# Pooling each batch row in its own 32 by 32 tile of TensorE, with a second gather of the fields as the weights and a matmul with ones as the sum

## The reference

```python
e = jnp.stack([tbl_0[ids[:, 0]], ..., tbl_32[ids[:, 32]]], axis=1)      # 512 x 33 x 128
row, col = np.triu_indices(33, k=1)
inner = x[:, row] * x[:, col]                                           # 512 x 528 x 128
fm = jax.nn.relu(jnp.einsum('bpd,ad->bpa', inner, attn_W) + attn_b)
scores = jnp.einsum('ba,bpa->bp', gnn_feature, fm)
attn = jax.nn.softmax(scores, axis=1)
attn_output = jnp.einsum('bp,bpd->bd', attn, inner) * 100.0
h = jnp.concatenate([gnn_feature, attn_output, r_gnn_feature], axis=1)
h = jnp.maximum(h @ W_top1 + b_top1, 0.0)
h = jnp.maximum(h @ W_top2 + b_top2, 0.0)
y = h @ W_top3
```

## Time and profile before

| | |
|---|---|
| median of 3 runs | 608.61 us (608.36 to 609.79) |
| the profiled execution: its own time, its span | 609.33 us, 607.5 us |
| TensorE matmul busy | 591.5 us (97%) |
| DVE busy | 567.9 us (93%) |
| ACT busy | 504.0 us (83%) |
| POOL busy | 235.6 us (39%) |
| share of the chain that ended last | PE 80%, DVE 10%, issue 3%, DMA 3%, ACT 2% |

### The profile page before, as it was taken

One profiled execution on the slowest core, in us unless ns is written; L12 is line 12 of the kernel. 1 busy time (PEld: TensorE's weight loads), 2 busy tenths in 40 slices (PEclk: granted clock), 3 DMA queues, 4 the chain that ended last, 5 costly groups with the idle time before them and its releaser, 6 DMA issues.

```text
span 607.5 us, 24776 instructions
## 1 busy us (share of the span) xinstructions
PE 591.5 (97%) x10754; PEld 401.6 (66%) x10754; DVE 567.9 (93%) x793; ACT 504.0 (83%) x1068; POOL 235.6 (39%) x215
## 2 busy tenths in 40 slices
PE   7999999999989999999999999999899999999887
PEld 5555555556669899555567789655467777556456
DVE  5699999999989999999999999999999999999963
ACT  2889899889988878889999878898899878887841
POOL 6688878864323333444423333443100122021010
PEclk9999999999999999999999999999999999999999
DMA  3212311151341113100071111200030011510250
GB/s 96 55 40 93 92 33 41 37 29 21 22 30 22 38 30 30 15 21 15 20 29 26 35 35 30 20 19 2 3 12 13 14 19 18 12 19 14 10 25 8
DMA packets 70189, 17.36 MB, mean 29 GB/s; under 512 B 66289, under 2 KB 67329, under 8 KB 70082
## 3 DMA queue, kind: packets, MB, share of 16 engines
q1 hardware_dynamic: 63634, 6.53, 13.9%
q0 software_dynamic: 4256, 8.68, 6.5%
q10 hardware_dynamic: 2192, 0.57, 0.5%
HBM read 13.84 MB, written 1.92 MB: 26 GB/s over the span
## 4 chain that ended last, share of the span: by engine, by line
PE 80%; DVE 10%; issue 3%; DMA 3%; ACT 2%; POOL 1%; SPq 1%; DVEq 0%; ACTq 0%
PE x_ps L578 63%; PE s_ps L606 7%; DVE inner L903 4%; PE m_ps L658 4%; DVE fm L916 4%; ACT rel L836 2%; PE s_ps L599 2%; PE m_ps L650 1%; DMA band_scratch<-attn 1%; PE s_ps L734 1%; PE x_ps L734 1%; DVE attn_out L1006 1%; POOL rows L473 1%; DMA idx_in<-in_ids 0%; DVE pooled L999 0%
## 5 line engine op out<-in xcount | busy, mean ns | idle before, releaser
L836 ACT ACTIVATE rel<-x_ps,shift,size 128x264 f32<-128x264 f32 x1024 | 489.1, 587 | 73.2 <-PE x_ps L578 60.1
L578 PE MATMUL x_ps<-inner,attn_w_t 128*32 128x264 f32 x8192 | 486.6, 387 | 7.4 <-DVE inner L903 5.4
L578 PEld LDWEIGHTS x_ps<-inner,attn_w_t 128*32 128x32 f32 x8192 | 299.1, 110 | 160.0 <-DVE inner L903 11.7
L903 DVE TENSOR_TENSOR inner<-e_t 128x1056 f32<-128x1056 f32 x256 | 314.0, 1266 | 0.7 <-PE x_ps L578 0.5
L473 POOL DMA_INDIRECT rows<-in_table,idx x128 | 163.0, 1273 | 194.3 <-PE s_ps L606 158.8
L916 DVE SCALAR_TENSOR_TENSOR fm<-rel,turn_sign 128x528 f32<-128x528 f32 x228 | 172.2, 783 | 14.9 <-ACT rel L836 11.3
L501 POOL TENSOR_TENSOR band<-band 128x192 f32<-128x192 f32 (+2 forms) x39 | 32.0, 820 | 114.5 <-DMA band<-band_scratch 114.0
L606 PE MATMUL s_ps<-fm,diag 128*32 128x264 f32 x912 | 75.7, 386 | 0.0
L606 PEld LDWEIGHTS s_ps<-fm,diag 128*32 128x32 f32 x912 | 34.9, 110 | 16.2
L658 PE MATMUL m_ps<-band,rows 128*32 128x132 f32 x896 | 35.5, 276 | 0.0
L658 PEld LDWEIGHTS m_ps<-band,rows 128*32 128x32 f32 x896 | 31.1, 109 | 3.6
(11 more groups left out here) (86 smaller groups left out, 128.7 us busy)
## 6 DMA issues: line engine op xcount, KB each, us to landing
band<-band_scratch SPq DMA_DIRECT2D x128, 18.4 KB, 1.8
rows<-in_table,idx POOLq DMA_INDIRECT x128, 3.0
band_scratch<-attn SPq DMA_DIRECT2D x32, 32.0 KB
band_scratch<-rows SPq DMA_DIRECT2D x1, 784.0 KB, 3.5
w<-in_W_top ACTq DMA_DIRECT2D x2, 256.0 KB, 3.8
w<-in_W_top SPq DMA_DIRECT2D x1, 512.0 KB
band_scratch<-attn SPq DMA_DIRECT2D x32, 1.0 KB
band<-band_scratch SPq DMA_DIRECT2D x24, 12.2 KB, 1.9
```

The source lines that it names most:

```text
L578: mm = pe.matmul(strip(x_ps[:, 2 * a + p, 0:HALF], c), strip_of(attn_w_t, 2 * p + c % 2), inner[:, slot, h, PAIR_ROWS * a + c // 2, :], st ...
L836: act.activation(rel[:, n % 2, a, p, h, :], x_ps[:, 2 * a + p, 0:HALF], ACT.Relu, bias=shift[:, p, c:c + 1], scale=size[:, p, c:c + 1]).th ...
L903: dve.tensor_tensor(inner[:, n % 2, h, :, :].rearrange("p q (i k) -> p q i k", k=HALF_HOPS), flat(e, at, [[P * WIDE, P], [WIDE, QUADS], [1 ...
```

## The change

- **Pooling on TensorE.** A set is now eight groups. Each of the four rows of a group has its own tile of 32 partitions by 32 columns: the weights are that row's folded band (32 fields by 32 fields, column 0 left out), and what streams is that row's 32 gathered fields, 128 columns. Groups with an even number use the diagonal tiles and the first of two PSUM banks, those with an odd number the tiles one column strip further and the second bank. The sets run in steps 5, 7, 9 and 11.
- **Weighing.** The result has (row, field) on the partitions and the embedding on the free axis. It is weighed by `out_rows`, a second indirect gather of fields 1 to 32 from the table (128 more gathers of 128 rows on POOL), 1024 elements a partition in one DVE instruction, into one buffer `pooled`.
- **Summing.** TensorE sums over fields by a matmul with ones (`picks`, 128 x 32 weights, 128 columns, one for each group) into `s_ps`; after a tile DVE copies the sums (`attn_rows`), TensorE turns them with one 128 x 128 matmul, and DVE copies them to `attn_out`.
- **Bands.** Pairs with field 0 are stored a second time, mirrored, by single elements (`store_flipped`); half stages are stored 64 rows at once, and loaded 16 groups at once. Folds are two for each tile. The late band is folded by DVE.
- **Others.** Step 12 leaves `FULL_AT` in three tiles. The copies to the other half are two of 64 partitions in place of four of 32. `tail_band` and its clearing on POOL (line 551) are gone; the rows have two buffers in place of three. The last part's layer 3 has a bank of its own and does not wait for the one before.

```diff
 FULL_AT = ((0, 1, 17),
-           (1, 12, 17),
-           (1, 12, 17),
-           (1, 12, 17, 25, 31))
+           (1, 17),
+           (1, 17),
+           (1, 17, 25, 31))
...
+        def store_flipped(queue, row, rows_of_attn, h, n, done):
+            pairs = HALF_HOPS if h else HALF_HOPS - 1
+            first = FIELDS - HALF_HOPS * (h + 1)
+            at = HALF_HOPS * first + HALF_HOPS - 1
+            queue.dma_start(flat(band_dram, row * BAND + first, [[BAND, n], [1, pairs]]),
+                            rows_of_attn[:, at:at + (HALF_HOPS - 1) * (pairs - 1) + 1:HALF_HOPS - 1],
+                            allow_slow_non_contiguous=True).then_inc(done, 16)
...
-            for store in (store_main, store_turned_around):
-                for a in range(DUOS):
-                    for h in range(SIDES):
-                        at = 32 * (SIDES * a + h)
-                        store(queue, REGION_ROWS * r + 32 * a, attn[at:at + 32, r, :], h, 32, band_stored)
+            for store in (store_main, store_turned_around, store_flipped):
+                for h in range(SIDES):
+                    store(queue, REGION_ROWS * r, attn[REGION_ROWS * h:REGION_ROWS * (h + 1), r, :], h, REGION_ROWS,
+                          band_stored)
...
-                    pool.memset(tail_band[:, :, :, :], 0.0).then_inc(tail_band_cleared, 1)
...
+            def pool_set(t, k):
+                if t == LAST and k == 0:
+                    pe.wait_ge(attn_out_ready, LAST)
+                if t == LAST and k == LATE_SET - 1:
+                    pe.wait_ge(late_attn_ready, 1)
...
+                if 1 <= k < (REGION_SETS if t == LAST else TILE_SETS):
+                    pe.wait_ge(pool_read, TILE_SETS * t + k)
+                pe.wait_ge(folded, SIDES * t + (2 + k - LATE_SET + 1 if k == LATE_SET else k // REGION_SETS + 1))
+                banks = set_banks(t, k)
+                first, end = set_groups(t, k)
+                for g in range(first, end):
+                    u, at = g % TWISTS, (g - first) // TWISTS * P
+                    for r in range(GROUP):
+                        part = slice(SIDE * r, SIDE * (r + 1))
+                        mm = pe.matmul(strip(banks[:, u, at:at + P], (r + u) % GROUP),
+                                       band[part, g // REGION, g % REGION, 1:FIELDS],
+                                       rows[part, t % BUFFERS, g, :], start=True, stop=True)
+                mm.then_inc(pool_done, 1)
...
+            def sum_set(t, k):
...
+                for g in range(first, end):
+                    at = SUM_ONES - GROUP * (g // GROUP)
+                    mm = pe.matmul(strip(sums_psum(t), g % GROUP), picks[:, at:at + STRIP], pooled_group(g, first),
+                                   start=g < GROUP, stop=g >= last - GROUP)
+                mm.then_inc(pool_summed, 1)
+
+            def turn_sums(t):
+                pe.wait_ge(sums_read, t + 1)
+                pe.matmul(turned_sums_psum(t), attn_rows[:, :], picks[:, PERM:PERM + P],
+                          start=True, stop=True).then_inc(sums_turned, 1)
...
-            for k in range(EARLY_SETS - 1):
-                pool_open(k)
+            pool_set(LAST, REGION_SETS)
             mlp_layer2(T2)
...
+            pool_set(LAST, LATE_SET - 1)
+            for k in range(REGION_SETS, LATE_SET):
+                sum_set(LAST, k)
             mlp_layer2(T01, (0,))
...
+            turn_sums(LAST)
             mlp_layer3(T2)
+            pool_set(LAST, LATE_SET)
+            sum_late_set()
             mlp_layer1(T3)
...
+            def weigh_set(t, k):
+                first, end = set_groups(t, k)
+                n, at = (end - first) // TWISTS * P, (first - first % SET + first % SET // TWISTS) * P
+                dve.wait_ge(pool_done, TILE_SETS * t + k + 1)
+                dve.wait_ge(out_gathered[first // SET], 16 * SET * (t + 1))
+                if TILE_SETS * t + k >= 1:
+                    dve.wait_ge(pool_summed, TILE_SETS * t + k)
+                dve.tensor_tensor(pooled[:, :, 0:n], set_banks(t, k)[:, :, 0:n],
+                                  flat(out_rows[:, :, :], at, [[STEPS * P, P], [SET // TWISTS * P, TWISTS], [1, n]]),
+                                  ALU.mult).then_inc(pool_read, 1)
```

440 lines of the change are left out of this document (221 added, 219 removed).

## The result

The changed kernel takes 622.02 us (median of four runs, 618.97 to 624.37), the kernel before 608.49 on the same chip: a ratio of 1.023, with an interval of 1.019 to 1.027. The forecast was 606.7. On another chip the same kernel came out at 1.0385 (1.0354 to 1.0415) and, on a chip on which the kernel before takes 649 us, at 1.1325.

What follows compares the result with a forecast made beforehand. TensorE, 97% busy, was taken as the bound, with DVE close behind. Terms -3.2 - 2.5 - 1.7 - 1.2 + 3.9 + 1.4 - 0.5 + 1.5 + 0.4 = -1.9 us took 608.6 to 606.7 us; range 601 to 615.

Steps and rivals of the forecast that it cites:

- Stores: Mirrored single elements, 960 a stage: 3.3 us more in the tail, covered in mid tile by several steps of slack.
- its own term for them: Instructions that come late because DMA traffic doubles around the stores: +0.4 us, bounds -1.7 and 3.
- the clock: Behind TensorE's idling ahead of the tail's band, granted clock falls to 0.50: +1.5 us, bounds 0 and 3.
- A set on TensorE: Pool set on 32 by 32 tiles, eight at once: 0.9 us plus 0.25 for changing the tiling, 1.15 us.
- DVE and clearing: Fewer DVE stalls of TensorE, -2.5 us (bounds 0 and 3); POOL's clearing of tail_band gone, -1.7 (bounds 0 and 1.8).
- The second gather: 128 further gathers at most double POOL's 39% busy share; each stands several steps ahead of its use.
- The band in the tail: Folded band reaches TensorE 3.9 us later; work behind it up to the last layer 1 takes 1.4 us more.
- Four tiles at a time: Rival: only four tiles run at once, a set costs 0.9 us more, +14, 620.6 us; chance 0.14, in-between cases included.
- one row tile a bank: Rival: row tiles writing one PSUM bank take turns, a set takes 3.6 us, +42, 649 us; chance 0.04.
- The tail not later: Rival: mirrored stores hide behind the others' landing, 3.9 falls to 0.6, no clock drop, 601.9 us; chance 0.12.
- The last tile's half band: Rival: band late for step 23's set if stores take 4 us more; 1.3 us of slack, 612 us; chance 0.08.

Runs made afterwards that it cites:

- the packed kernel: Changed kernel with mirrored pairs written side by side by DVE and stored as 128 pieces a stage, not 960 single elements: 613.7 us, 1.0106 of before.
- the combined kernel: The packed kernel with gathers placed otherwise, stores reordered, four matmuls keeping TensorE at work in the tail, and tail sums behind other work: 615.45 us, 1.0115 of before.
- one gather in four: Changed kernel with the second gather made for tile 0 alone, 32 of 128 gathers left: 630.95 us, 1.0352 of before.

## Why the prediction was wrong, step by step

- **Stores: the step that failed.** The prediction charged the mirrored elements with 3.3 us in the tail and nothing in mid tile, where "several steps of slack" covered them. The slack covers the band, and the band was not late there. What was late are instructions: its own term for them, +0.4, had an upper bound of 3. Measured, the single elements cost 18 of 23 us (packed against not, 632.15 and 613.7), and some 6 when they are added to the kernel before, in two runs. In the profiled run the steps' excess is 3.1, 1.4 and 2.0 us in the step 5s (1.7 before, in tile 1 alone), 1.1 and 4.1 in step 21 of tiles 1 and 3, by lateness and the clock behind it. How the elements make instructions late stays open: the fetches of the kernels without them are as slow. By stretches, the steps miss the forecast by 13.6 us (+5.4 for -8.2) and the tail by 2.7; the packed kernel's steps, at -2.1, still miss it by 6.1.
- **A set on TensorE.** Right in tile 3: 1.20 for 1.15. In tiles 1 and 2, beside gathers, 1.31 to 1.34, which no term had: over all sets some 1.7 us. Sums (0.43 to 0.44 for 0.45) and turn (0.53 for 0.5) as forecast.
- **DVE and clearing.** Right: the waits for DVE fell from 5.4 to 1.8 us, step 20 of tile 1 takes 4.06 for 4.51, step 29 of tile 2 4.13 for 5.79, step 29 of the last tile 4.97 for 6.42. In the kernel before, the clearing's stall could not be had alone: moved, it came back in another step.
- **The second gather.** "Busy twice as long at most" was right, 401 us for 236, but the cover was thinner than that share says. GpSimd's copies of the wrapped fields came late in tile 0: step 31 is 5.39 us for 4.0, 1.4 us that no term had.
- **The band in the tail.** From the last scores to the set TensorE sees 10.3 us for 4.6: 5.7 later, where 3.9 was forecast; the loads start 3.0 later, and the late rows' stores now meet them. Behind it, the clock costs 2.5 us for 1.5 forecast, and the rest of 14.0 - 9.9 us is 1.5, for 1.4. The end gives back 0.7, for 0.5. That the mirrored elements' 3.3 us nearly make the sum is partly luck: the kernel without them has a tail only 2.6 us shorter and still 6.4 longer than before, with loads 1.4 later, which no term had.
- **Rivals.** Four tiles at a time, one row tile a bank: refuted. The tail not later: refuted. The last tile's half band was late by 0.39 us at the set of step 23, no more, and the combined kernel lost 4.6 us there with one fold behind three gathers: that step is near its edge.

What remains open: why the packed kernel, 4.4 us above before, still loses 2.0, 0.7 and 0.3 us in the step 5s of tiles 1 to 3 and 1.2, 0.5 and 1.4 in their step 21. Main stores of 4096 pieces of 32 bytes and 1024 single elements are in both kernels, and the kernel before shows such a stall too, 1.70 us in step 5 of tile 1. Whether keeping gathers away from the stores helps on an ordinary chip was not settled, though the wait of 2.25 us above came without any. No kernel here beats the one before.

## What to carry to other kernels

Count a transfer by its pieces, not by its bytes or its landing: 960 writes of 4 bytes a stage cost more than five times the 3.3 us that their landing promised, mostly on an engine that never waited for them. Pack strided elements with an instruction of a compute engine before they are stored. Where TensorE has no slack, look at the steps during and behind a burst of small writes for waits that name nobody, and leave nothing that it needs behind a gather in GpSimd's queue.

## What the hardware did that I had not expected

- Beside small writes other transfers are slow. Instruction fetches of 16 KB took 1.04 us in a quiet stretch and 2.2 among the stores, and single ones up to 2.7 in the kernel before and 3.7 in the packed one. The waits for issue fall on the same instructions in different kernels: the seventh of step 5 in tile 1 (before, changed, and before with more stores), the 22nd of step 21 in the last tile (changed, one gather in four). That fits a boundary between two fetches; how much a slow fetch delays TensorE was not measured.
- The 64 matmul instructions of a set start within 0.885 us in tile 3, one in 14 ns as the earlier trace rows suggested, but within 1.00 to 1.03 us in tiles 1 and 2, where gathers run beside them: even on an ordinary chip a dense set seems to feel them.
- The clock falls behind a wait of 2.08 us in one run and not in another (the earlier trace rows and the row above), and stays at 0.50 for 3.4 us or 10.2.
- Chips differ more than tenfold in what gathers cost beside dense TensorE work: 0.11 to 0.14 us in the step of a set on one chip (5.75 to 5.78 in tiles 1 and 2 against 5.64 in tile 3), 2.3 on another (7.94 against 5.64).
